# Start-up of a fused decoder layer: a semaphore for each early load, the weight split in parts, and a new order on TensorE and VectorE

## What is computed

```
L, D = 112, 256;  batch 32;  context length 375
h  = ln(ln(x)) * norm_w + norm_b                # two normalisations
q, k, v = split(h @ qkv_w.T + qkv_b)            # 256 columns each
w  = softmax(q^T (k / sqrt(L)))                 # 256 x 256, over channels, for each sample
x1 = x + (v w^T) @ proj_w.T + proj_b + ln(x)
x2 = x1 + cross_attention(ln(x1), ctx)          # similarity 112 x 375, softmax, W_l
out = x2 + moe(ln(x2))                          # 8 experts, 4 chosen per token, one shared
```

## Time and profile before

| | us |
|---|---|
| median of 3 runs | 748.32 (746.50 to 749.77) |
| profiled execution | 747.58 |
| its span in the profile | 745.8 |
| granted TensorE clock, mean over the span | 0.983 |

### The profile page before, as it was taken

How to read it: one execution, slowest core, us unless ns; L and a number is a source line. 1 busy time by engine, 2 the same in 40 slices (tenths; PEclk the granted TensorE clock), 3 DMA queues, 4 the chain that set the end, 5 groups by cost and what they waited for, 6 DMA issues and landing times. The chain is left out here.

```text
span 745.8 us, 12056 instructions
## 1 busy us (share of the span) xinstructions
PE 697.2 (93%) x4072; PEld 588.4 (79%) x4072; DVE 449.7 (60%) x1174; ACT 358.0 (48%) x859; POOL 199.3 (27%) x290
## 2 busy tenths in 40 slices
PE   3999999999999999999999866999999999999997
PEld 2867878778788788788787754788888888888886
DVE  5575655755654646557556665766666667666432
ACT  3755663665656556646665323434242333333331
POOL 2142221314204305223141302232223222232222
PEclk9999999999999999999999887999999999999999
DMA  7505024033051060240420266022222212131200
GB/s 210 155 22 165 6 76 141 0 111 103 0 163 51 22 186 6 77 137 0 123 66 1 75 203 218 1 113 85 115 85 113 86 41 107 50 121 50 114 29 29
DMA packets 50765, 64.43 MB, mean 86 GB/s; under 512 B 3800, under 2 KB 49416, under 8 KB 49840
## 3 DMA queue, kind: packets, MB, share of 16 engines
q1 hardware_dynamic: 50736, 64.06, 27.3%
HBM read 56.60 MB, written 7.45 MB: 86 GB/s over the span
## 5 line engine op out<-in xcount | busy, mean ns | idle before, releaser
L1381 POOL TENSOR_TENSOR sg<-sg,cw_wide 128x512 f32<-128x512 f32 x56 | 73.9, 1319 | 186.6 <-ACT sg L1338 177.0
L1342 ACT ACTIVATE a_hi<-af 128x512 fp32r<-128x512 f32 x63 | 39.8, 632 | 155.8 <-DVE af L1462 155.8
L75 PE MATMUL bank<-h_hi,w_lo 128*128 128x512 f32 x224 | 92.4, 412 | 6.5 <-DVE w_lo L1479 4.7
L76 PE MATMUL bank<-h_lo,w_hi 128*128 128x512 f32 x224 | 90.0, 402 | 0.0
L77 PE MATMUL bank<-h_hi,w_hi 128*128 128x512 f32 x224 | 89.6, 400 | 0.0
L1462 DVE TENSOR_TENSOR af<-bank,sg 128x512 f32<-128x512 f32 x63 | 43.2, 686 | 62.0 <-POOL sg L1381 58.9
L1467 DVE TENSOR_TENSOR a_lo<-af,a_hi 128x512 fp32r<-128x512 f32 x63 | 48.1, 763 | 34.9 <-ACT a_hi L1342 34.9
L75 PE MATMUL bank<-w_hi,a_lo 128*128 128x256 f32 x224 | 63.2, 282 | 0.0
L76 PE MATMUL bank<-w_lo,a_hi 128*128 128x256 f32 x224 | 63.2, 282 | 0.0
L77 PE MATMUL bank<-w_hi,a_hi 128*128 128x256 f32 x224 | 63.1, 282 | 0.0
L844 POOL TENSOR_TENSOR x2b<-x,bl_wide 112x256 f32<-112x256 f32 x32 | 23.1, 753 | 146.6 <-DMA x_scratch<-x2b 146.6
(11 more groups left out here) (226 smaller groups left out, 1901.0 us busy)
## 6 DMA issues: line engine op xcount, KB each, us to landing
cw_wide<-cw_scratch SPq DMA_DIRECT2D x7, 2048.0 KB, 7.1
ctxtf<-in_ctx_t SPq DMA_DIRECT2D x32, 375.0 KB
ctxf<-in_ctx SPq DMA_DIRECT2D x32, 375.0 KB
xt<-in_x SPq DMA_DIRECT2D x8, 448.0 KB, 8.1
x_scratch<-x2b SPq DMA_DIRECT2D x8, 448.0 KB, 10.7
x2n<-x_scratch SPq DMA_DIRECT2D x7, 512.0 KB, 4.8
x2t<-x_scratch SPq DMA_DIRECT2D x7, 512.0 KB, 4.1
out_dram<-x2t SPq DMA_DIRECT2D x7, 512.0 KB, 2.9
```

The lines of the kernel that those rows point to most:

```text
L75: pe.matmul(dst, a_lo, b_hi, start=first, stop=False, **kw)
L76: pe.matmul(dst, a_hi, b_lo, start=False, stop=False, **kw)
L1342: act.activation(a_hi[n % (AHEAD + 1)][:, :], af[(p + n) % 2][:, :], ACT.Copy).then_inc(a_hi_ok, 1)
L1381: pool.tensor_tensor(sg[b][:, :], sg[b][:, :], cw_wide[p][:, ORDER[n], :], ALU.mult).then_inc(sgw_ok, 1)
```

## The change

- Loads: norm_w and norm_b have a semaphore of their own (`norm_in`), the weights keep `w_in`, the identity has `ident_ok`, the two biases `bias_in`. The identity is issued behind the weights instead of ahead of them.
- Weight split: VectorE makes each low part as soon as ScalarE's high part is there (`w_high`, `w_low` in the place of `w_split`), ahead of h.
- VectorE: nb_wide and nwq wait for the norm weights alone. Behind the low parts come the sum of the bias product, then rows 0, 1, 2 of h, h_low(0), row 3, h_low(1) to h_low(3), then the scaling and the bias rows.
- TensorE: the q/k bias product first, then the four transposes. The v bias product comes behind the q/k products 0 and 1, whose bias-row matmuls come behind it. v_product(0) has its place between q/k product 2 and 3 in group 0 too (ScalarE's v_copy(0) likewise).

```diff
--- before.py
+++ after.py
...
             cx_in = [sem(f"context{j}_in") for j in range(G)]
+            norm_in, ident_ok, bias_in = sem("norm_weights_in"), sem("identity_in"), sem("biases_in")
             wide = sem("nb_widened")
             nwq_ok, qk_bias_ok = sem("q_norm_scale"), sem("qk_bias_sum")
-            w_split, wp_hi_ok, wp_lo_ok = sem("qkv_weights_split"), sem("proj_weights_hi"), sem("proj_weights_lo")
+            w_high, w_low, wp_hi_ok, wp_lo_ok = sem("qkv_weights_hi"), sem("qkv_weights_lo"), sem("proj_weights_hi"), sem("proj_weights_lo")
             wl_hi_ok, wl_lo_ok = sem("l_weights_hi"), sem("l_weights_lo")
...
-            QKV_LOADS, EARLY_LOADS, LATE_LOADS = 6, 3, 5
-            QKV_SPLITS = 2 * 2 * KB
+            EARLY_LOADS, LATE_LOADS = 3, 5
+            QKV_SPLITS = 2 * KB
             qkv_parts = [(slice(0, D), nwq), (slice(D, 3 * D), nw)]
...
                 sp.dma_start(xt[:, :, :], x_tiles[:, 0:G, :]).then_inc(x_in, 16)
-                sp.dma_start(ident[:, :], ident_in).then_inc(w_in, 16)
-                sp.dma_start(nw[:, :], norm_w).then_inc(w_in, 16)
-                sp.dma_start(nb[:, :], norm_b).then_inc(w_in, 16)
+                sp.dma_start(nw[:, :], norm_w).then_inc(norm_in, 16)
+                sp.dma_start(nb[:, :], norm_b).then_inc(norm_in, 16)
                 sp.dma_start(wqkv_f[:, :, :], qkv_wt.rearrange("(k p) n -> p k n", p=P)).then_inc(w_in, 16)
-                sp.dma_start(qk_bias0[:, :], qk_b.partition_broadcast(L)).then_inc(w_in, 16)
-                sp.dma_start(v_bias0[:, :], v_b).then_inc(w_in, 16)
+                sp.dma_start(ident[:, :], ident_in).then_inc(ident_ok, 16)
+                sp.dma_start(qk_bias0[:, :], qk_b.partition_broadcast(L)).then_inc(bias_in, 16)
+                sp.dma_start(v_bias0[:, :], v_b).then_inc(bias_in, 16)
                 def load_context(batch, j):
...
-                sp.wait_ge(w_split, QKV_SPLITS)
+                sp.wait_ge(w_low, QKV_SPLITS)
                 sp.wait_ge(vbias_mm, 1)
...
-                for j in range(G):
-                    turn_h(j)
                 pe.wait_ge(wide, 1)
-
+                pe.wait_ge(w_in, 16)
                 for k in range(KB):
...
                 last.then_inc(bias_mm, 1)
-                for half in range(KB):
-                    for k in range(KB):
-                        last = pe.matmul(v_bank[1][:, half:half + 1], wqkv_f[:, k, 2 * D + half * P:2 * D + (half + 1) * P],
-                                         nb[:, k:k + 1], start=(k == 0), stop=(k == KB - 1))
-                last.then_inc(vbias_mm, 1)
+                pe.wait_ge(ident_ok, 16)
+                for j in range(G):
+                    turn_h(j)
...
+                def v_bias_product():
+                    for half in range(KB):
+                        for k in range(KB):
+                            last = pe.matmul(v_bank[1][:, half:half + 1], wqkv_f[:, k, 2 * D + half * P:2 * D + (half + 1) * P],
+                                             nb[:, k:k + 1], start=(k == 0), stop=(k == KB - 1))
+                    last.then_inc(vbias_mm, 1)
+
                 def group(i, last_group):
...
-                    def qk_product(j):
+                    def qk_main(j):
                         pe.wait_ge(h_lo_ok, ev[j])
...
                                 wqkv_lo[:, k, 0:2 * D], k == 0, False)
-                        if j == 0 and is_first(i):
-                            pe.wait_ge(rows_ok, 1)
+
+                    def qk_row(j):
                         pe.matmul(bank[j][0:L, :], two_ones[:, :], qk_rows[:, :], start=False, stop=True).then_inc(qk_mm, 1)
+
+                    def qk_product(j):
+                        qk_main(j)
+                        qk_row(j)
...
-                    qk_product(0)
-                    qk_product(1)
+                    if is_first(i):
+                        qk_main(0)
+                        qk_main(1)
+                        v_bias_product()
+                        pe.wait_ge(rows_ok, 1)
+                        qk_row(0)
+                        qk_row(1)
+                    else:
+                        qk_product(0)
+                        qk_product(1)
                     qk_product(2)
-                    if not is_first(i):
-                        v_product(0)
+                    v_product(0)
                     qk_product(3)
...
                     scores(3)
-                    if is_first(i):
-                        v_product(0)
                     v_product(1)
...
-                pe.wait_ge(w_split, QKV_SPLITS)
+                pe.wait_ge(w_low, QKV_SPLITS)
                 group(0, False)
...
                     qk_copy(2)
-                    if not is_first(i):
-                        v_copy(0)
+                    v_copy(0)
                     qk_copy(3)
...
                     probs_high(1)
-                    if is_first(i):
-                        v_copy(0)
                     exps(3)
...
                 act.wait_ge(nwq_ok, 1)
+                act.wait_ge(w_in, 16)
                 for k in range(KB):
                     for n, scale in qkv_parts:
-                        act.activation(wqkv_hi[:, k, n], wqkv_f[:, k, n], ACT.Copy, scale=scale[:, k:k + 1]).then_inc(w_split, 1)
+                        act.activation(wqkv_hi[:, k, n], wqkv_f[:, k, n], ACT.Copy, scale=scale[:, k:k + 1]).then_inc(w_high, 1)
                 for j in range(G):
...
+                def normalise_row(j):
+                    dve.tensor_scalar(hh[:, j, :], xt[:, j, :], mv1[:, j, 0:1], ln1[:, 6, j:j + 1], ALU.subtract,
+                                      ALU.mult).then_inc(hh_ok, 1)
+
                 def normalise_h(g):
...
                     for j in range(G):
-                        dve.tensor_scalar(hh[:, j, :], xt[:, j, :], mv1[:, j, 0:1], ln1[:, 6, j:j + 1], ALU.subtract,
-                                          ALU.mult).then_inc(hh_ok, 1)
+                        normalise_row(j)
...
                 ln1_moments(0)
-                dve.wait_ge(w_in, 16 * QKV_LOADS)
+                dve.wait_ge(norm_in, 32)
                 dve.tensor_copy(nb_wide[:, :, :], nb[:, :].unsqueeze(2).to_broadcast([P, KB, L])).then_inc(wide, 1)
...
                 dve.wait_ge(nwq_ok, 1)
-
-
-                normalise_h(0)
-                dve.wait_ge(w_split, QKV_SPLITS // 2)
                 for k in range(KB):
-                    for n, scale in qkv_parts:
+                    for part, (n, scale) in enumerate(qkv_parts):
+                        dve.wait_ge(w_high, 2 * k + part + 1)
                         dve.scalar_tensor_tensor(wqkv_lo[:, k, n], wqkv_f[:, k, n], scale[:, k:k + 1], f32(wqkv_hi[:, k, n]),
-                                                 ALU.mult, ALU.subtract).then_inc(w_split, 1)
-                for j in range(G):
-                    h_low(j)
+                                                 ALU.mult, ALU.subtract).then_inc(w_low, 1)
                 dve.wait_ge(bias_mm, 1)
+                dve.wait_ge(bias_in, 32)
                 dve.tensor_tensor(qk_bias[:, :], m_bank[0:L, :], qk_bias0[:, :], ALU.add).then_inc(qk_bias_ok, 1)
+                dve.wait_ge(ln1_step, LN1_STEPS)
+                normalise_row(0)
+                normalise_row(1)
+                normalise_row(2)
+                h_low(0)
+                normalise_row(3)
+                h_low(1)
+                h_low(2)
+                h_low(3)
                 dve.wait_ge(qk_bias_ok, 1)
```

## The result

The changed kernel takes 750.86 us (median of 8 runs, 749.48 to 753.69) against 747.75 for the kernel before (8 runs, 746.22 to 749.77). The ratio is 1.0042, 95% interval 1.0028 to 1.0056: slower by 3.1 us. The forecast was 747.7, with 745.2 to 750.2 as its range; the loss is under the 0.5% bound, but it lies outside the range and on the other side. The profiled execution took 750.05, its span 748.1 (745.8 before).

A forecast was written before the change was run, and what follows sets the result against it. TensorE, busy 93%, bounds the whole run, but the start-up chain bounds what the change touches. Scores 0.45 earlier, up to 0.3 more from the clock, 0.6 taken: 747.7 from the median 748.32, range 745.2 to 750.2.

The forecast's parts named there:

- Loads: Start-up: weights issued one slot earlier, at 2.20 instead of 2.67, land at 7.9, bounds 7.7 and 8.17.
- The bias sum: VectorE in the start-up: sum comes at 11.6, when the bias product begun at 7.95 releases its reader.
- First q/k matmul: TensorE in the start-up: first q/k matmul at 15.1, 2.1 earlier than 17.21.
- the bias rows: At qk_row(0): bias rows ready at 18.05, TensorE arrives at 18.9, so the 0.55 wait is gone, 0.85 to spare.
- v_product(0): Group 0, now ahead of the scores: its 1.24 is paid, and idle time before probs_proj(0) grows by it.
- a rival for the clock in the start-up: Start-up: TensorE's clock rises only at 17.7, q/k matmuls from 15.1 lose 1.3, giving 749.0; chance 0.17.
- an idle TensorE of about 2 us: Sign that the forecast is right: TensorE idles about 2 us before probs_proj(0).
- My case: Main forecast: scores and probs_proj(0) 0.6 earlier, later work moves with them, 747.7 on the median; chance 0.52.
- The row at 742 to 744 us: Evidence against the clock rival: an idle TensorE kept full clock for most of 742 to 744, 0.90 over it.
- Contention: GpSimd's last ln1 steps beside VectorE's low parts: 0.22 for each of four, ending at 11.7, under 12.3; cover 0.6.
- Sum: Scores at 23.9 instead of 24.35, 0.45 earlier, up to 0.3 more from faster transposes; 0.6 taken.
- the rivals: Late clock 749.0, GpSimd held longer 749.1, v_product(0) free 746.5, loads unmoved 748.0, or something far off over 3.7 us.

The follow-up runs named there:

- the changed kernel with six matmuls: Changed kernel plus six unused matmuls in TensorE's idle time before probs_proj(0) of group 0: 749.56 us, ratio 1.0027.
- the new orders: Changed kernel with v_product(0) back, early table load, v bias product behind q/k one, h rows before bias sum: ratio 0.9986; plus 16 unused start-up matmuls: 0.9973, 0.9981.
- the loads alone: Kernel before with only the new load semaphores and the identity issued behind the weights, engine orders as before: 748.44 us, ratio 1.0008.
- v_product(0) moved, six matmuls added: Kernel before with v_product(0) of group 0 ahead of q/k product 3 and six unused matmuls before probs_proj(0): 749.42 us, ratio 1.0019.
- Cutting the pause to 0.84: Changed kernel with the v bias product straight behind the q/k bias product, in TensorE's pause before the transposes: 750.18 us, ratio 1.0026.
- the warm-up: 16 unused matmuls on TensorE from 2.3 us, added to the reordered start-up with v_product(0) back: ratio 0.9973, on another chip 0.9981.

## Why the prediction was wrong

*Loads, right.* Weights at 7.76 (forecast 7.9, and 7.5 to 8.8 over the ten profiles with the early load). The bias sum began at 11.93 (11.6): the table load of 1.28 us, put by the program in front of the first activation and so behind the new second wait, held the high parts until 9.05; I had left it out, though it cost no more than 0.3 here. First q/k matmul 14.85 (15.1). TensorE's first row matmul did not wait for the bias rows, as forecast.

*v_product(0), half right.* "1.24 is paid, and the idle time before probs_proj(0) grows by it": both came, with 1.78 us of idle time. The failed step is that I priced this idle time at nothing beyond its own length. The forecast has a rival for the clock in the start-up and none for the clock here, though it named "an idle TensorE of about 2 us" as a thing to be seen. It costs 1.48.

*The clock in the start-up.* The rival to which I gave 0.17 came true in its price: forecast loss 1.3, measured 4.42 - 2.8 = 1.6. Its mechanism, a rise that comes late, is not what this profile shows: the clock had risen before the transposes and fell at 15.65. Two other profiles with the very same start-up program do show a late rise: v_product(0) back, and the changed kernel with six matmuls. The first has its transposes at half speed,

```profile
13.58 1.35 PE L364 MATMUL bank<-ident,h 112*128 112x112 f32 x6 [1.54 <-DVE h L889]
```

and the 12 q/k matmuls took 3.83 and 4.84 in the two, a loss of 1.0 and 2.0. That 1.3 lies so near 1.6 is luck. My case needed a full clock from 15.1 on. The row at 742 to 744 us was no support for it: it shows that the clock stays up in an idle time, and not what comes behind one. In the changed kernel the clock reads 1.00 from 30 to 32 us as well, and then it falls.

*Contention, right in kind and size.* GpSimd's steps L819 and L820 took 0.72 and 0.32 instead of 0.20 each beside the low parts and ended at 11.41, ahead of the first row of h at 12.53. The rule of the Trainium skill (GPSIMD Engine Reference, section 8, Key points) holds with 0.64 us for the two. In the new orders, where rows of h wait for it, it becomes part of the path: the last step began at 11.61 in the first of them, and at 10.64 with the loads alone.

*Sum.* 0.6 forecast as gain at the scores, 0.73 measured as loss: of the 1.3 between them 1.6 is the first fall, less what the earlier q/k start gave back. Behind it the 1.48, which makes 2.8. The whole error is 3.7 (0.6 gained forecast, 3.1 lost measured; the base of three runs, 748.32, was 0.57 above the median of eight and hides that much of it). The last 0.9 no profile shows: the two profiled spans differ by 2.3, and the interval of the ratio begins at 2.1. In the range I had added the rivals one at a time; the first fall alone, 749.0, was inside, both together were not.

*Left open.* What decides the first fall. With one and the same order of the start-up TensorE comes to full speed at different times: with the order of the kernel before, the bias product took 3.62 us in two profiles and 2.70 and 2.78 in two others, and in one of the first two (v_product(0) moved, six matmuls added) the first six q/k matmuls, from 18.04, still went at 0.43. Cutting the pause to 0.84 did not keep the q/k matmuls fast; with the warm-up they were fast in three profiles of four. What is shown is that it comes and what it cost in each profile, not a rule for when.

## What to carry to other kernels

Ask of every move what it leaves idle behind it: here an idle time of 1.8 us on TensorE cost, beside itself, 1.5 us by half speed behind it, where later pauses of 1.5 us cost only themselves. Work that lay in the shadow of another engine's chain kept the clock up and was free there; ahead of that chain it was paid in full. And when a semaphore is split, look for the wait that ends last behind it (here GpSimd's ten steps), and for a table load that a new wait pushes onto the path.

## What was not expected of the hardware

The granted clock of the windows reads 1.00 where it has not yet risen for the first time. In the changed kernel with v_product(0) back:

```profile
16.00:17.00 1.00, 1.00 (x4) 0.73 (x3) 0.55 (x2) 0.94 (x3) 0.00 (x0) 1.00 1.15 231
18.00:19.00 1.00, 1.00 (x6) 0.76 (x5) 0.62 (x2) 0.38 (x1) 0.00 (x0) 1.00 1.00 188
```

Both rows show 1.00, but the pitch of the same matmuls is 0.43 in the first and 0.23 in the second. Before the first change that a trace shows, only the pitch tells the clock. And the same early load, issued at 2.20 us each time, landed between 7.5 and 8.8 us in different executions, a spread of 1.3 us that is as large as what most of these edits are worth.
